# Eight transformer blocks in one kernel: the variance add of each layer norm moves from VectorE to GpSimd

## The reference

```
def _layernorm(x, axis=-1, eps=1e-05):
    m = jnp.mean(x, axis=axis, keepdims=True)
    v = jnp.var(x, axis=axis, keepdims=True)
    return (x - m) / jnp.sqrt(v + eps)
...
x = x + _L0_attn_ref(_layernorm(x, axis=-1), ...)   # causal attention, 16 heads
x = x + _L0_ffn_ref(_layernorm(x, axis=-1), ...)    # 8 experts, the best 2 of them
x = x + _L1_attn_ref(_layernorm(x, axis=-1), ...)   # linear attention with 64 relu features
x = x + _L1_ffn_ref(_layernorm(x, axis=-1), ...)    # 16 experts, the best 1, and a shared one
x = x + _L2_attn_ref(_layernorm(x, axis=-1), ...)   # banded attention
x = x + _L2_ffn_ref(_layernorm(x, axis=-1), ...)    # 32 experts, the best 4 of them
x = x + _L3_attn_ref(_layernorm(x, axis=-1), ...)   # convolution, a scan over 48 states, gated MLP
x = x + _L3_ffn_ref(_layernorm(x, axis=-1), ...)    # squared relu, then spike counts
```

## Time and profile before

| | us |
|---|---|
| median of 3 runs | 1874.7 |
| lowest, highest | 1870.06, 1875.76 |
| the profiled execution's own time | 1870.06 |
| its span, first to last instruction | 1868.1 |

### The profile page before, as it was taken

One profiled execution on the slowest core, in us unless ns is written; L12 is line 12 of the kernel. 1 busy time (PEld: TensorE's weight loads), 2 busy tenths in 40 slices (PEclk: granted clock), 3 DMA queues, 4 the chain that ended last, 5 costly groups with the idle time before them and its releaser, 6 DMA issues.

```text
span 1868.1 us, 28958 instructions
## 1 busy us (share of the span) xinstructions
PE 1597.8 (86%) x10611; PEld 919.3 (49%) x10660; DVE 1279.8 (69%) x2913; ACT 1023.6 (55%) x1967; POOL 776.3 (42%) x670
## 2 busy tenths in 40 slices
PE   7789989877988899987798889997678888999867
PEld 4457763313555676431355567542135556754214
DVE  5555548997655465799865455599966555559996
ACT  4464446655555444665556544566545654456654
POOL 2321116785232112578614220178831422117891
PEclk9999999978999999998899999998879999989979
DMA  6004402120000440212000054021100005302110
GB/s 225 1 1 143 139 16 69 33 86 13 12 1 2 144 136 10 74 47 73 12 12 1 13 157 117 12 91 47 51 12 6 1 26 158 108 6 91 46 52 12
DMA packets 91982, 105.41 MB, mean 56 GB/s; under 512 B 7104, under 2 KB 70336, under 8 KB 91584
## 3 DMA queue, kind: packets, MB, share of 16 engines
q1 hardware_dynamic: 89792, 99.37, 17.4%
q0 software_dynamic: 2048, 4.20, 0.7%
HBM read 80.60 MB, written 22.94 MB: 55 GB/s over the span
## 4 chain that ended last, share of the span: by engine, by line
PE 52%; DVE 23%; ACT 11%; issue 6%; POOL 6%; DMA 2%; DVEq 0%; SPq 0%; ACTq 0%; POOLq 0%
PE P L236 10%; DVE M L2036 9%; PE P L1650 4%; PE P L1879 4%; PE P L1231 2%; POOL M L2106 2%; PE P L1247 2%; PE P L404 2%; PE P L1236 2%; PE P L976 2%; DVE st L185 2%; PE P L1826 2%; PE P L2164 2%; ACT P L1971 1%; PE P L218 1%
## 5 line engine op out<-in xcount | busy, mean ns | idle before, releaser
L2036 DVE TENSOR_TENSOR_SCAN M<-P,M 128x512 f32<-128x512 f32 x384 | 443.2, 1202 | 24.6 <-ACT P L1971 24.1
L1971 ACT ACTIVATE P<-M,negA 128x512 f32<-128x512 f32 x384 | 262.3, 689 | 169.9 <-DVE M L2036 167.7
L236 PEld LDWEIGHTS P<-wt,M 128*128 128x128 f32 x2176 | 276.9, 195 | 115.6 <-issue 34.5
L236 PE MATMUL P<-wt,M 128*128 128x128 f32 x2176 | 297.0, 283 | 21.7 <-DVE M L1747 5.3
L1879 PE MATMUL P<-M,wt 32*32 32x512 f32 x3072 | 237.4, 690 | 87.7 <-DVE M L2036 64.5
L2106 POOL TENSOR_TENSOR M<-M 128x512 f32<-128x512 f32 x192 | 238.3, 1273 | 96.2 <-ACT M L1953 74.6
L2106 POOL TENSOR_TENSOR M<-W,M 128x512 f32<-128x512 f32 x192 | 243.6, 1299 | 43.2 <-PE P L1879 42.6
L210 POOL TENSOR_TENSOR st<-st,wt 128x4 f32<-128x4 f32 x64 | 66.0, 1031 | 216.7 <-DVE st L194 206.3
L1879 PEld LDWEIGHTS P<-M,wt 32*32 32x32 f32 x3072 | 38.9, 109 | 232.5 <-DVE M L2036 163.8
L1650 PE MATMUL P<-M,wt 128*128 128x512 f32 x256 | 133.0, 601 | 2.9 <-ACT M L1708 1.7
L1747 DVE TENSOR_TENSOR M<-M,P 128x512 f32<-128x512 f32 x128 | 85.8, 675 | 67.1 <-PE P L1658 48.6
(11 more groups left out here) (352 smaller groups left out, 3186.8 us busy)
## 6 DMA issues: line engine op xcount, KB each, us to landing
W<-in_e SPq DMA_DIRECT2D x88, 192.0 KB, 2.6
M<-in_e SPq DMA_DIRECT2D x64, 192.0 KB, 2.7
M<-dt SPq DMA_DIRECT2D x48, 256.0 KB, 4.6
M<-xs SPq DMA_DIRECT2D x32, 256.0 KB, 3.0
ys<-M SPq DMA_DIRECT2D x32, 256.0 KB, 2.4
W<-du SPq DMA_DIRECT2D x32, 256.0 KB, 4.9
W<-xh SPq DMA_DIRECT2D x16, 256.0 KB
M<-du SPq DMA_DIRECT2D x16, 256.0 KB, 4.6
```

Source lines behind the costliest of these rows:

```text
L236: m = e.matmul(out[:, tok(j)], h[:, tok(j)], wgt, start=first and j == 0, stop=last, skip_group_check=True)
L1971: e.activation(t["aa"][n % 2][:, :], t["dtr"][i][:, :], EXP, scale=negA[:, c:c + 1]).then_inc(ACT.s, ACT.mark(b, "a3", "aa", n))
L2036: e.tensor_tensor_scan(bb[:, :], t["aa"][n % 2][:, :], bb[:, :], 0.0, MUL, ADD).then_inc(DVE.s, DVE.mark(b, "a3", "scan", n))
```

## The change

The add of 1e-5 leaves `dve_norm` and becomes a step of its own in `pool_norm`. POOL now waits for "mv" instead of "var", adds, yields, waits for its own mark "var" and takes the power. The four turn tables for tensor, scalar, vector and gpsimd are new; the one for gpsimd has 682 turns where it had 618. The table for sync is the same.

```diff
@@ dve_norm
             w.wait_ge(DVE.s, DVE.of(b, tag, "mv"))
             mean = st[:, 24:32].rearrange("p (j c) -> p j c", c=2)[:, :, 0]
-            var = st[:, 24:32].rearrange("p (j c) -> p j c", c=2)[:, :, 1]
-            e.tensor_scalar(st[:, 32:36], var, 1e-5, None, ADD).then_inc(DVE.s, DVE.mark(b, tag, "var"))
             if tag == "a3":
                 e.tensor_scalar(st[:, 0:4], mean, -1.0, None, MUL).then_inc(DVE.s, DVE.mark(b, tag, "neg"))
             yield
@@ pool_norm
             w.wait_ge(w_in[0], 16)
-            w.wait_ge(DVE.s, DVE.of(b, tag, "var"))
+            w.wait_ge(DVE.s, DVE.of(b, tag, "mv"))
+            var = st[:, 24:32].rearrange("p (j c) -> p j c", c=2)[:, :, 1]
+            e.tensor_scalar(st[:, 32:36], var, 1e-5, None, ADD).then_inc(POOL.s, POOL.mark(b, tag, "var"))
+            yield
+            w.wait_ge(POOL.s, POOL.of(b, tag, "var"))
             e.tensor_tensor(st[:, 36:40], st[:, 32:36], wv("mhalf")[:, 0:4], POW).then_inc(
                 POOL.s, POOL.mark(b, tag, "rstd"))
@@ TURNS
             "tensor": (2211,
-                "4334000c708091176c2ceffff50fe1000002891081ee4f8ff1f3c673d90c90d97fe10fc2f867aa000800000013bea57b41f7"
+                "0000010007944ddbf0a6fffff50fe1000004489081de8ff1d1ef9a75d90c90cd7fe10fc2f867a6001000000007bc5d7b21f7"
...
-            "gpsimd": (618,
+            "gpsimd": (682,
...
```

More of the change, by code:

```diff
@@ L2264, in program @@
             "tensor": (2211,
-                "4334000c708091176c2ceffff50fe1000002891081ee4f8ff1f3c673d90c90d97fe10fc2f867aa000800000013bea57b41f7"
-                "e97f73b7f3ebf1e9bf0017ff85d61229ff1725001edac20003daff87677fffac383c4608000093c0f727fcac7be18e50c30d"
-                "2ffe117c370f3de710000030a78038be15187f6dee7f6f3eef67a6d70115f859f81497ff1729001ed9640003daffc36b7fff"
-                "fa87f0800002082c40f799fe55f6c37798d28078bff84386f0ea980704000001d3c3e0f6237fe9fdcfcf7afba7a67b013c7f"
@@ L2269, in program @@
-                "0b9e120dff174c000f5fa000d94bfbf616ddfffa87f0800002083840f727f53e5de0ce3d8e480f7ffe10e17c336648000002"
-                "e003c3e0f6761ff56ef7cf5eefc7a63f0127f7fffff09e8507afe"),
-            "scalar": (1644,
[L2272 to L2276, removed]
@@ L2277, in program @@
-            "vector": (2247,
[L2278 to L2283, removed]
@@ L2284, in program @@
-            "gpsimd": (618,
-                "9330c3f05e30c00000000a8023ffffffbffbef8cfc03fc13ccc00000000d0800ffffcfffff7fe33f0c7d05e3140000000648"
-                "003ffffffbeffbf8cfc30fc178c60000000290800ffffffffffff2c"),
+                "0000010007944ddbf0a6fffff50fe1000004489081de8ff1d1ef9a75d90c90cd7fe10fc2f867a6001000000007bc5d7b21f7"
+                "6de7fd7babf7e0f93f8017ffe0ce0549ff079a001ed9460003daff86cbfffed8780f2608000053c0f7fc98f3f01ece90c30e"
+                "57fe11785f0f3de6a000000c6e800f3c95187f6fceefdcf3dfc7a5b7020bfe14f812a7ff0799001ebe500005daffc36dbfff"
@@ new lines, in program @@
+                "fa87f0800001083840f797d9aeb1f39bd8e48078bff08785f0f2a801c1000000f3c3e0fd287fe7af9fb77df3c7a4f71e0a3f"
+                "0d9c0a66ff07ac001ebe6000bb0bfbde167dfffa87f08000010821c0f787cf83f371b69d8e480f7ff087e17c336702000000"
+                "03cf03e0fd307ff3cfe79fcff3c7a55f18257ffffff09b8507b7e"),
+            "scalar": (1644,
+                "000018c65318f6ff69dcc008a4005bdd6ef7be422279039d6b482047b98a1440c9122a4512821426fcfbf7fffffbeafba721"
+                "22c7cc1c013dd01ffdeac8971802290bf6cd9fb238c93e0496eb73209bb354411112488a510a48a0abfac57fbffefb5ff58b"
+                "5ac8b1f9d0004f7479b7fb4eea00441202dfb37bbf728223d013bb10e482dfa6c08444a2449449222427f6a66fffefff5ebf"
+                "69a991387bd801173ab7367f93ba80110480b77cdb7b5d940af2073acb5040bbf1b0221149122522848909dafa57ffdfffff"
+                "fffe8e824ff"),
@@ new lines, in program @@
+            "vector": (2247,
+                "0000003ffe1e101ce00000016bfa009e7fff5ff2bf8101800800c483f3f93fffff03181e026050c00df4100e3ffc2ffc6221"
+                "9222285a7f34001f15e8fdf7ffffa5b073fe021f01f4b8c3ffe1f21cfc20000002944fd7d7effbfeff8140808000a1403f3f"
+                "ff027eff4c5027920ac07f27aa087e9ffe0c450c182894cfee0007a079f665fffe55e173ffe6017c07b3a18fff87c83bf800"
+                "000146fe80dd7ffdf7e5fe040c040020923f0ff0fffffc06a2180b800a601fd1ed023fffd92d0184a425327f38003a81fbfb"
+                "ecfc7fecb06cffe003f03d8e863ffff0ff21800000c10bfa0375fff7df97f8102410000a143f0fcfffffd831887106003c00"
+                "7f573801fffee8cc0c60286499fce000ad07dbfdfffffffffc1f98037fe07e"),
@@ L2287, in program @@
+            "gpsimd": (682,
+                "01fc1c2fc0c78e0e0000000071004ffffffeffee7f0cff003ff031e38e00000000e80103ffffbff7fcffc33fc1c2fc0dc8e1"
+                "c0000000720080ffffffdfefcff0cff070bf036638700000000e80013fffffffffffccc"),
             "sync": (191,
```

## The result

The changed kernel takes 1888.1 us in the median of 5 runs (1883.86 to 1891.09), beside 1872.88 of the kernel before, now in 5 runs as well; the ratio is 1.0076, with a 95% interval from 1.0054 to 1.0097. By this ratio it is slower by 14 us, where 1868 and a gain of 6.7 were forecast; the range ended at 1881. All ratios in this document leave out two executions that took far longer than their kernels' others, one of e4 (5073 us) and one of e15 (3022 us).

A forecast was written before the change was run, and what follows sets the result against it. No engine was full; PE held 52% of the chain that ended last, DVE 23%. 1870.06 - 5.2 - 1.5 + 0 + 0 = 1863.4, or 1868.0 on the median's scale (1874.7 - 6.7); range 1855 to 1881.

The forecast's parts named there:

- Term A: Variance adds leaving DVE: gain of 5.2 us from the adds on the chain, bounded by 0 and 10.6.
- The blocked adds: DVE variance adds held up beside POOL's 128x2048 memset: six took about 1.81 us, four of them on the chain.
- the 0.48 of L1140: Next DVE instruction behind a blocked add would end 0.48 us earlier without it; four times, 1.9 us.
- rival 1: The DVE adds were hidden by other work, so only 1 to 4 us are gained, 1872; chance 0.35.
- Term C: Adds and own waits put on POOL's norm arm: net cost 0, from 0 to +28 us.
- the 2.2 us of small pieces: Part of the DVE gain: 22 variance adds on the chain, 0.17 us at most each, summing to 2.2.
- The two signs named for this term: On POOL, an add mean over 0.35 us, or idle DVE before the scaling that POOL ends in most norms.
- Term B: Kernel start, lane 0's norm ahead of lane 1's memsets and transposes: gain of 1.5 us if postponed work finds room.
- the sign named for this: PE busy less than before in the first 51 us would prove the forecast gain at the start wrong.
- rival 3: New order costs time: lane 0 runs alone at the start, PE idles, loss up to 9 us, 1881; chance 0.10.
- Term D: Rest of the new turn order after the start: 0, between -8 and +9 us.
- Rival 4: POOL add at twice the DVE price, 0.34 us, some 6 us cost, net gain 1 us, 1873.5; chance 0.03.

The follow-up runs named there:

- e4: Kernel before, adds still on DVE, with the changed kernel's turn order up to about 81 us, then the old order; ratio 1.0028 to the kernel before.
- e15: Kernel before with the add of 1e-5 left out and the new turn order only from about 920 us on; ratio 0.9996 to the kernel before.
- e5: Kernel before with the add of 1e-5 left out altogether, old turn order; ratio 0.9971 to the kernel before.
- e12: Kernel before with POOL's 128x2048 memset of block a1 issued behind the norm's power instead of ahead of it; ratio 0.9982 to the kernel before.
- e2: Kernel before with the adds moved to POOL, directly ahead of their powers, old turn order; ratio 1.0021 to the kernel before.
- e6: Changed kernel with the add of 1e-5 left out altogether, new turn order; ratio 1.0038 to the kernel before.
- e8: Changed kernel with the POOL add done twice in each norm, the second waiting for the first; ratio 1.0131 to the kernel before.
- e3: Changed kernel with the old turn order up to about 81 us, then its own; ratio 1.0046 to the kernel before.
- e13: Kernel before with the add of 1e-5 left out and the new turn order only up to about 81 us; ratio 1.0010 to the kernel before.
- e14: Kernel before with the add of 1e-5 left out and the new turn order only from 81 to about 920 us; ratio 1.0014 to the kernel before.
- e1: Changed kernel's turn order with the adds kept on DVE in their own step, POOL's add step empty; 1913.3 us, ratio 1.0209 to the kernel before.
- e10: Kernel before with only POOL's first eight turns changed, putting lane 0's memsets and norm ahead of lane 1's memsets; ratio 1.0015 to the kernel before.
- e7: Changed kernel's turn order with the adds on DVE, each directly behind its aggregate; ratio 1.0083 to the kernel before.

## Why the prediction was wrong, step by step

- **Term A, the adds off DVE: right.** Forecast -5.2 us, measured -5.4 (e5, interval -7.5 to -3.3). The blocked adds and the 0.48 of L1140 behind four of them were read correctly (e12), and rival 1 (the adds were hidden, 1 to 4 us) hardly fits. But e5 takes more away than term A does, as POOL's arm has no add at all there.
- **Term C, what is added on POOL: the mis-sized term.** Forecast 0, measured +7.1 to +9.4 us; A and C together were to gain 5.2 and cost 3.9 (e2). "The arm on POOL now costs 0.08 to wake, 0.15, some 0.05 for the own wait": measured are 0.09, 0.23 and 0.08, together 0.40 where 0.28 stood on the other side, and the power 0.02 longer. The 0.15 was taken "nearest the memset" of 98 ns; the product of 128x64 at 298 ns was the nearer row. I had written of the two tied arms that whoever lengthens POOL's pays in full, and then took for the added piece the value at which it comes out even. A small gain was also counted twice: 0.4 of the 2.2 us of small pieces in term A stand on the chain directly in front of the power, and term C sets that same add on DVE against the new one. The two signs named for this term, a mean above 0.35 us and waits that POOL ends in most norms, did not appear (0.253 us, 20 of 64), and yet it was wrong: they were set too far out.
- **How term C comes about is shown in part.** From the aggregate to the end of the power the median is 1.13 us in e5 and 1.45 in e2, to the end of the centring 1.32 and 1.31. So without an add POOL's arm has 0.19 to spare, and the first add ends it 0.13 too late. From the aggregate to the scaling, summed over the 64 norms, e2 takes 141.7 us where e5 takes 136.9, and the changed kernel 148.4 where e6 takes 145.2: 3 to 5 us of the 7 to 9. The rest lies within the uncertainty and stays open. A second add finds nothing to spare: 157.7 (e8) less 148.4 is 9.3, beside 10.3 measured.
- **Term B, the start: wrong in sign.** Forecast -1.5, measured +5.2 (e4), +5.6 (changed against e3) and +7.3 (e13 against e5). Its first step held: counted from the landing of the weights, L200 was 0.93 us earlier (1.1 forecast) and PE's key projection 1.0 (1.5 forecast). The step that failed is the condition behind "L412 gains some 0.4 more, as PE does not wait for lane 1", that postponed work finds room later. PE did not wait for lane 1, it waited for lane 0's own DVE work, with nothing of lane 1 to fill the gap; it lost that work's place, and in six of seven profiles with this start and no fillers a part of its clock as well. PE busy less than before in the first 51 us was the sign named for this, and it came: 35.83 against 36.50, a part of it at the lower clock. That is rival 3, which I priced at up to 9 us by idle time alone and gave 0.10; against it I held "that stretch had lane 0 ahead already", which the PE rows of the changed order show to be no argument.
- **Term D, the rest of the order: inside its bounds, at the bad end.** Forecast 0 between -8 and +9. The whole order costs 12.5 us (e6 minus e5, 0.67%); less 5.2 to 7.3 for the start that leaves 5 to 7. e14 and e15 show it on both sides of 920 us; no single place was found, so its cause stays open.
- **The sum.** -5.4 + 7.1 + 12.5 = 14.2, the measured 14.2 (0.76%). This is no test: e5 and e6 each enter once with either sign, so it must come out. With the price of the add from the old order, 9.4, it is 16.5. The largest miss is the order, 12.5 where B and D had -1.5; the smaller one is term C. The errors had one sign: a cost set at nothing, a gain for an effect whose other half was not priced, and a spread centred on zero.
- Rival 4 (twice the DVE price, from the Trainium skill's "GPSIMD Engine Reference", 4.1 Engine selection) had the sign of term C right, and its 6 us came nearest. Its price was too high: an instance takes 0.228 in the median where DVE's took 0.170, 1.3 times. The page has its twice for operations with two inputs and roughly line rate for one input, and this add has one.

## What to carry to other kernels

Where two arms of a join end within 0.01 us, what makes either longer than it was is paid in every instance where that arm is last: price the piece by the nearest row of like shape, wait included, and count how often the arm is last. A reordering that runs one lane alone takes the filler out of PE's gaps; look at what PE does in each wait of the new order, and price a lowered clock behind the gaps beside the idle time. One profile is not enough for that: of two executions with nearly the same gaps one kept its clock and one did not. And when tables were laid out for one kernel, they are no neutral test for another (e1): fill the empty steps and look where they stand.

## What the runs showed of the hardware

- The short add of 128x4 takes 0.170 us in the median on DVE and 0.228 on POOL (0.141 and 0.216 at least, in e1 and e8); in the changed kernel POOL takes up a mark of DVE's 0.09 us after it, and its own 0.08 after, where ACT needs 0.04.
- DVE and POOL hold each other up also in scalings: in e12 a half of L202 takes 1.50 us beside a product of 1.26 on POOL (0.42 in the median). The Trainium skill ("SBUF — State Buffer", SBUF: two separate sides) has a DVE instruction with two inputs in SBUF and a GpSimd instruction that reads SBUF exclude each other for a whole instruction; 1.50 is the 1.26 and a part of its own 0.42, which agrees. A held add also holds what stands behind it on DVE: in e10 the scaling was done only with the add, at 10.50.
- PE's granted clock was 0.57 from 28 to 36 us in the changed kernel, behind gaps of 1.60, 1.37 and 0.68 us, and 1.00 in e7, behind gaps of 1.49, 1.36 and 0.68. Nearly the same gaps lowered the clock in one execution and not in another. With it lowered, the next block began 2.0 us later (48.9 against 46.9 us after the weights landed).
